# Holding back two late products and norming the last group tile by tile, at the end of a Mamba and LoRA layer kernel

## The reference

```
a   = layernorm(x)
h   = a + mamba2(rmsnorm(a))                   # stage A
mlp = h + down(silu(gate(rmsnorm(h))) * up(..))   # stage B, inner width 1792
x1  = x + layernorm(mlp)                       # stage C from here
h3  = layernorm(x1)
u   = h3 @ W_up.T + LoRA of the expert with the highest logit (4 experts, rank 8)
out = x1 + layernorm(u)
```

## Time and profile before

| | us |
|---|---|
| median of 3 runs (lowest, highest) | 816.61 (816.28, 816.96) |
| the profiled execution, its own time | 815.18 |
| its span, first to last instruction | 813.3 |
| TensorE matmuls busy | 762.6 (94%) |
| VectorE busy | 485.3 (60%) |
| ScalarE busy | 331.6 (41%) |
| GpSimd busy | 154.1 (19%) |

### The profile page before, as it was taken

One profiled execution on the slowest core, in us unless ns is written; L12 is line 12 of the kernel. 1 busy time (PEld: TensorE's weight loads), 2 busy tenths in 40 slices (PEclk: granted clock), 3 DMA queues, 4 the chain that ended last, 5 costly groups with the idle time before them and its releaser, 6 DMA issues.

```text
span 813.3 us, 13857 instructions
## 1 busy us (share of the span) xinstructions
PE 762.6 (94%) x5558; PEld 536.6 (66%) x5558; DVE 485.3 (60%) x1109; ACT 331.6 (41%) x603; POOL 154.1 (19%) x197
## 2 busy tenths in 40 slices
PE   3994989989999999999999999999999999999945
PEld 3863866668666876577666876677656866577622
DVE  6877567877644765467645765467635664265163
ACT  2643476625523363325523363325523463222201
POOL 1421121205110331115110331015110330010010
PEclk9896899999999999999999999999999999999987
DMA  9941000110103120210103020310103010111010
GB/s 325 387 160 26 2 27 1 32 47 5 49 1 65 40 52 1 49 57 13 40 1 79 27 53 1 52 53 25 30 1 78 27 27 1 27 53 27 1 52 27
DMA packets 59936, 41.11 MB, mean 51 GB/s; under 512 B 45664, under 2 KB 45792, under 8 KB 59872
## 3 DMA queue, kind: packets, MB, share of 16 engines
q1 hardware_dynamic: 59872, 40.22, 17.6%
HBM read 25.01 MB, written 4.19 MB: 36 GB/s over the span
## 4 chain that ended last, share of the span: by engine, by line
PE 85%; DVE 7%; ACT 2%; DMA 2%; issue 1%; SPq 1%; POOL 0%; POOLq 0%; DVEq 0%; ACTq 0%
PE gu L1251 34%; PE wa L1251 25%; PE acc L1251 18%; PE wc L1251 7%; DVE weights L870 2%; DMA weights<-in_w_in 1%; DVE sg L1043 1%; DVE stats_c L885 0%; PE wa L1274 0%; DVE h L1073 0%; DMA xa<-in_x 0%; DMA ht<-ra 0%; ACT act L680 0%; PE wc L1466 0%; ACT weights L560 0%
## 5 line engine op out<-in xcount | busy, mean ns | idle before, releaser
L1251 PE MATMUL gu<-h2t,weights 128*128 128x256 f16 x2688 | 313.4, 273 | 0.6 <-DVE h2t L1037 0.6
L1251 PEld LDWEIGHTS gu<-h2t,weights 128*128 128x128 f16 x2688 | 260.9, 98 | 56.1 <-issue 19.7
L1251 PE MATMUL acc<-weights,act 128*128 128x512 f16 x672 | 163.4, 379 | 6.5 <-DVE act L1048 6.5
L1043 DVE SCALAR_TENSOR_TENSOR sg<-gu,bound,sg 128x256 f32<-128x256 f32 x112 | 53.6, 479 | 122.6 <-ACT sg L670 121.9
L670 ACT ACTIVATE sg<-gu,scale_inv 128x256 f32<-128x256 f32 x112 | 52.9, 472 | 160.3 <-PE gu L1251 160.1
L1251 PE MATMUL wa<-ht,weights 128*128 128x256 f16 x912 | 110.4, 280 | 3.7 <-DMA ht<-ra 3.7
L1251 PEld LDWEIGHTS acc<-weights,act 128*128 128x128 f16 x672 | 65.3, 98 | 63.6 <-DVE act L1048 8.3
L1251 PEld LDWEIGHTS wa<-ht,weights 128*128 128x128 f16 x912 | 91.6, 101 | 22.4 <-DMA ht<-ra 4.0
L680 ACT ACTIVATE act<-sg 128x256 f16<-128x256 f32 x112 | 46.6, 416 | 88.7 <-DVE sg L1043 88.7
L1048 DVE TENSOR_TENSOR act<-sg,act 128x256 f16<-128x256 f32 x112 | 50.5, 451 | 54.0 <-ACT act L680 54.0
L943 DVE SCALAR_TENSOR_TENSOR xbc<-wa,conv_ws,xbc 128x253 f32<-128x253 f32 (+1 forms) x132 | 57.3, 475 | 10.2 <-ACT xbc L597 8.6
(11 more groups left out here) (194 smaller groups left out, 800.4 us busy)
## 6 DMA issues: line engine op xcount, KB each, us to landing
xa<-in_x SPq DMA_DIRECT2D x8, 512.0 KB, 3.6
weights<-in_x SPq DMA_DIRECT2D x8, 512.0 KB, 3.7
out_x<-h SPq DMA_DIRECT2D x16, 256.0 KB, 2.2
weights<-in_w_in SPq DMA_DIRECT2D x5, 512.0 KB, 7.0
weights<-in_w_down SPq DMA_DIRECT2D x3, 768.0 KB, 14.1
weights<-in_w_gate SPq DMA_DIRECT2D x2, 1024.0 KB, 12.3
weights<-in_w_up SPq DMA_DIRECT2D x2, 1024.0 KB, 13.8
weights<-in_w_gate SPq DMA_DIRECT2D x2, 768.0 KB, 13.8
```

Source lines behind the costliest of these rows:

```text
L1043: nc.vector.scalar_tensor_tensor(sg[:, f % 2], GU[f % 2][:, SEQ:2 * SEQ], up_to_act, sg[:, f % 2], ALU.mult, ALU.mult).then_inc(sem("prod_ ...
L1251: return nc.tensor.matmul(dst, left, right, start=start, stop=stop)
```

## The change

Four things change, in steps 8 and 9 only.

- Group 6's linear and LoRA products (`c_u(6, 0)` and `c_u(6, 1)`) leave blocks 10 and 11. TensorE makes them after the last down product, one after the other, into the banks `WA[0]` and `WA[1]`. Their copy on ScalarE, and `c_stats3(6)` and `c_out(6)` on VectorE, move behind the last block as well.
- Stage C of group 7 is written out in a function `last()` for each engine. Its norms go tile by tile, with the buffers `xa` (for x1), `hn` (for h3 and the output) and the small ones of stage A.
- Its transposes put all four column blocks of one tile in a bank; the split and the logits follow per tile. The linear product of tile 1 is cut in two halves, with the small transposes between them.
- SP loads x for group 7's stage C into `xa`, ahead of the stores of group 6.

The diff, cut to its core:

```
+def held(g):
+    return g == GROUPS - 2
 def u_bank(g, j):
-    return ACC[j] if alone(g) else WC
+    return ACC[j] if alone(g) else WA[j] if held(g) else WC
+def h3_of(g):
+    return hn if alone(g) else h3
+def x1_of(g):
+    return xa if alone(g) else x1
+T3_LAST = [WC, GU[0]]
+LAST = GROUPS - 1
...
 @block.sync
     def c_x(g):
-        if g > 0:
+        if alone(g):
+            sp.wait_ge(sem("h0_ready"), g * 2 + 2)
+        elif g > 0:
             sp.wait_ge(sem("out_ready"), g * 2)
         if g == 0:
             wait_split(sp, order)
-        sp.dma_start(x1[:], x_g[g]).then_inc(xc_loaded, 16)
+        sp.dma_start(x1_of(g)[:], x_g[g]).then_inc(xc_loaded, 16)
...
+        if b is not None and alone(b):
+            c_x(b)
         if c is not None:
             c_store(c)
-        if b is not None:
+        if b is not None and not alone(b):
...
 @block.gpsimd
-        nc.gpsimd.tensor_tensor(dst, dst, c_half[:, 0:TILES], ALU.pow).then_inc(ready, 1)
+        nc.gpsimd.tensor_tensor(dst, dst, c_half[:, 0:dst.shape[1]], ALU.pow).then_inc(ready, 1)
...
+    def last_norm(n, j, scale):
+        pool.wait_ge(sem("last_stats_ready"), 2 * n + j - 1)
+        inv_std(chain_last, s_a[:, 0, j:j + 1], mv_a[:, j, 1:2], 1.0 / scale ** 2, EPS / scale ** 2,
+                sem("last_rstd_ready"))
...
+    def last():
+        chain_last.group(0)
+        for j in range(TILES):
+            last_norm(1, j, 1.0)
+        for j in range(TILES):
+            last_norm(2, j, ACT_SCALE)
+        norm_c(LAST - 1, 3, 1.0)
+        chain_c.close()
+        for j in range(TILES):
+            last_norm(3, j, 1.0)
+        chain_last.close()
...
 @block.scalar
+    def last_t3(j):
+        eng.wait_ge(sem("last_t3_ps_ready"), j + 1)
+        eng.wait_ge(sem("u_ps_ready"), LAST * 2)
+        nc.scalar.activation(h3t[:, 0, :, j * P:(j + 1) * P], T3_LAST[j][:].rearrange("p (k q) -> p k q", k=KB),
+                             ACT.Copy).then_inc(sem("last_t3_hi"), 1)
...
+    C_AT = {4: lambda g: c_hi3(g), 7: lambda g: c_zt(g),
+            10: lambda g: held(g) or c_u(g, 0), 11: lambda g: held(g) or c_u(g, 1)}
...
+    def last():
+        for j in range(TILES):
+            c_u(LAST - 1, j)
+        for j in range(TILES):
+            last_t3(j)
+        c_zt(LAST)
+        for j in range(TILES):
+            c_u(LAST, j)
...
 @block.vector
+    def last_stats(src, j):
+        chain_last(nc.vector.bn_stats(stats_a[:, j], src[:, j]))
+        nc.vector.bn_aggr(mv_a[:, j], stats_a[:, j]).then_inc(sem("last_stats_ready"), 1)
+    def last_center(n, j, src, ready):
+        dve.wait_ge(sem("last_rstd_ready"), 2 * n + j - 1)
+        nc.vector.tensor_scalar(hn[:, j], src[:, j], mv_a[:, j, 0:1], s_a[:, 0, j:j + 1],
+                                ALU.subtract, ALU.mult).then_inc(ready, 1)
+    def last_x1(j):
+        last_center(1, j, mlp, sem("last_n1_ready"))
+        if j == 0:
+            dve.wait_ge(xc_loaded, GROUPS * 16)
+        dve.wait_ge(sem("last_n1_ready"), j + 1)
+        nc.vector.tensor_tensor(xa[:, j], xa[:, j], hn[:, j], ALU.add).then_inc(sem("last_x1_ready"), 1)
+        dve.wait_ge(sem("last_x1_ready"), j + 1)
+        last_stats(xa, j)
+    def last_t3(j):
+        dve.wait_ge(sem("last_t3_hi"), j + 1)
+        nc.vector.tensor_tensor(h3t[:, 1, :, j * P:(j + 1) * P], T3_LAST[j][:].rearrange("p (k q) -> p k q", k=KB),
+                                h3t[:, 0, :, j * P:(j + 1) * P], ALU.subtract).then_inc(sem("last_t3_split"), 1)
+    def last_out(j):
+        last_center(3, j, hn, sem("last_n3_ready"))
+        dve.wait_ge(sem("last_n3_ready"), j + 1)
+        nc.vector.tensor_tensor(hn[:, j], hn[:, j], xa[:, j], ALU.add).then_inc(sem("out_ready"), 1)
...
+    C_AT = {0: lambda g: c_stats1(g), 1: lambda g: c_x1(g), 3: lambda g: c_stats2(g), 4: lambda g: (c_h3(g), c_lo3(g)),
+            6: lambda g: c_route(g), 12: lambda g: held(g) or c_stats3(g), 13: lambda g: held(g) or c_out(g)}
...
+    def last():
+        chain_last.group(0)
+        for j in range(TILES):
+            b_mlp(LAST, j)
+            dve.wait_ge(sem("mlp_ready"), LAST * 2 + j + 1)
+            last_stats(mlp, j)
+        for j in range(TILES):
+            last_x1(j)
+        for j in range(TILES):
+            last_center(2, j, xa, sem("last_h3_ready"))
+        c_stats3(LAST - 1)
+        chain_c.close()
+        for j in range(TILES):
+            last_t3(j)
+        chain_c.group(LAST)
+        c_route(LAST)
+        c_out(LAST - 1)
+        for j in range(TILES):
+            dve.wait_ge(sem("u_ready"), LAST * 2 + j + 1)
+            last_stats(hn, j)
+        for j in range(TILES):
+            last_out(j)
+        chain_last.close()
...
 @block.tensor
+    def last_t3(j):
+        pe.wait_ge(sem("last_h3_ready"), j + 1)
+        if j == 0:
+            pe.wait_ge(sem("zt_ready"), LAST * 2)
         else:
+            pe.wait_ge(sem("prod_ready"), LAST * FBLK + FBLK - 1)
+        for k in range(KB):
+            last = nc.tensor.transpose(T3_LAST[j][:, k * P:(k + 1) * P], hn[:, j, k * P:(k + 1) * P], ident[:])
+        last.then_inc(sem("last_t3_ps_ready"), 1)
...
     def c_logits(g):
-        if alone(g):
-            pe.wait_ge(sem("h3t_ready"), 2)
-        else:
+        if not alone(g):
             pe.wait_ge(h3t_loaded, g * 32 + 32)
             prev(g, 2, 2, pe, sem("u_ready"))
         if g + 2 < GROUPS:
             pe.wait_ge(sem("dtv_ready"), g + 3)
         n = E + E * R
         for j in range(TILES):
+            if alone(g):
+                pe.wait_ge(sem("last_t3_split"), j + 1)
...
+    def c_linear(g, j, ks=range(KB)):
+        split_product(u_bank(g, j)[:], [tokens(h3t, k, j) for k in ks],
+                      [[Wh[:, S_LIN + k, s] for s in range(2)] for k in ks], start=ks[0] == 0, stop=False)
...
     def c_u(g, j):
-        if alone(g):
+        if j == 0:
             pe.wait_ge(sem("zt_ready"), g * 2 + 2)
-        elif j == 0:
-            pe.wait_ge(sem("zt_ready"), g * 2 + 2)
-            c_linear(g, j)
-        else:
+        elif not held(g):
             pe.wait_ge(sem("u_ready"), g * 2 + 1)
-            c_linear(g, j)
+        c_linear(g, j)
         c_lora(g, j)
...
+    def last():
+        for j in range(TILES):
+            c_u(LAST - 1, j)
+        for j in range(TILES):
+            last_t3(j)
+        c_logits(LAST)
+        pe.wait_ge(sem("mlp_ready"), GROUPS * 2)
+        c_linear(LAST, 0)
+        c_linear(LAST, 1, (0, 1))
+        c_zt(LAST)
+        c_linear(LAST, 1, (2, 3))
+        pe.wait_ge(sem("zt_ready"), GROUPS * 2)
+        for j in range(TILES):
+            c_lora(LAST, j)
...
+    C_AT = {6: lambda g: c_logits(g), 7: lambda g: c_zt(g),
+            10: lambda g: held(g) or c_u(g, 0), 11: lambda g: held(g) or c_u(g, 1)}
```

More of the change, by code:

```diff
@@ L503, in norm_c @@
                         sem("rstd_c_ready"))
+            def last_norm(n, j, scale):
+                pool.wait_ge(sem("last_stats_ready"), 2 * n + j - 1)
+                inv_std(chain_last, s_a[:, 0, j:j + 1], mv_a[:, j, 1:2], 1.0 / scale ** 2, EPS / scale ** 2,
+                        sem("last_rstd_ready"))
             def step(a, b, c):
+                if c is not None and alone(c):
+                    return
                 if c is not None:
@@ L522, in step @@
                     a_rms(a)
-                if c is not None:
+                if c is not None and not held(c):
                     norm_c(c, 3, 1.0)
                     chain_c.close()
+            def last():
[9 more added lines that the diff above has]
+                chain_last.close()
             def first():
@@ L538, in _ @@
             steps(step)
+            last()
         @block.scalar
@@ L710, in _ @@
             NEXT_AT = {10: lambda g: a_hi1(g), 13: lambda g: a_conv(g, 0)}
-            C_AT = {4: lambda g: (c_t3(g, 0), c_t3(g, 1)) if alone(g) else c_hi3(g), 7: lambda g: c_zt(g),
-                    10: lambda g: c_u(g, 0), 11: lambda g: c_u(g, 1)}
+            C_AT = {4: lambda g: c_hi3(g), 7: lambda g: c_zt(g),
[8 more added lines that the diff above has]
+                    c_u(LAST, j)
             def step(a, b, c):
+                if c is not None and alone(c):
+                    return
                 if a is not None:
@@ L1049, in b_lo, with b_mlp @@
                     .then_inc(sem("act_ready"), 1)
-            def b_mlp(g):
-                if g == 0:
+            def b_mlp(g, j):
+                if g == 0 and j == 0:
                     wait_split(dve, order)
[L1054 to L1058, removed]
-                    else:
-                        dve.wait_ge(sem("down_done"), g * FBLK + FBLK)
-                    nc.vector.scalar_tensor_tensor(mlp[:, j], ACC[j][:], inv_down, h1b[:, j], ALU.mult, ALU.add)\
-                        .then_inc(sem("mlp_ready"), 1)
+                if j == 0:
+                    dve.wait_ge(sem("h1b_ready"), g + 1)
+                    prev(g, 32, 32, dve, h3t_loaded)
```

(20 more changed lines are left out.)

47 lines of the change are left out of this document (8 added, 39 removed).

## The result

The changed kernel took 806.27 us, the median of 4 runs (805.04 to 807.84), against 816.64 for the kernel before in the same session: a ratio of 0.9875, 95% interval 0.9859 to 0.9891, so 10.4 us less. The forecast was 806.6. A second session (6 runs, 804.55 to 808.73, before 815.15) gave 806.28, ratio 0.9892 (0.9874 to 0.9909). The runs of the changed kernel scatter by 2.8 us in the first session and by 4.2 in the second; those of the kernel before do so as well, by 3.4 us beside the first experiments (813.77 to 817.17).

The account below looks back on a forecast made before the run. TensorE's products bound the kernel until the last down products, then the order of work across engines in the last 31 us. Gains 7.47 + 0.8 + 1.1 + 1.2 + 0.4 = 11.0, less 1.1 for clock, about 10.0: 806.6 us, range 804.6 to 809.1.

Parts of the forecast that it names:

- Held products: Group 6's late products leave TensorE before the last down product: 6.25 us, plus 1.2 from VectorE's queue.
- Norms by tile: Last group's norms one tile at a time: 0.8 us gained up to the centred tiles, 0.4 at the end.
- GpSimd beside VectorE: Roots on GpSimd stretch beside VectorE work in the last group's norms: 1.0 us together, bounds 0 and 1.3.
- Transposes, split, logits: Last group, centred pair to end of logits: 3.2 us instead of 4.3, 1.1 gained, with group 6's statistics in between.
- Last products: TensorE works through 24 linear and 2 LoRA products after the logits; stretch before first output shortens by 1.2 us.
- The clock: TensorE's granted clock falls in the thin tail and returns at 789.7, losing 1.1 us; bounds 0 and 2.6.
- rival B: Clock falls and stays low until 792.6 in the tail, costing 2.6 us: 808.2 us; chance 0.12.
- rival A: Clock holds through the tail: 805.6 us, or 804.6 with roots unstretched; chance 0.33.
- The argument from the pause of 2.51 us: A 2.51 us TensorE pause earlier in the trace, between dense work, did not lower the clock.
- Moved DMAs: Reload of x on SP's queue ahead of group 6's stores, issued about 742, some 36 us early: free.
- Rival D: Reload of x stays stuck on SP behind group 6's stores: 18 us lost, 11 gained, 823.6 us; chance 0.02.
- Rival C: Tile by tile brings nothing because each hand-over to GpSimd stands open: 7.5 of 10.0 left, 809.1 us; chance 0.09.

Follow-up runs that it names:

- the first experiments: The session in which norms in pairs, fill, statistics later and a kernel without held products ran beside the kernel before, which took 815.25 us.
- fill: Changed kernel plus ten unread matmuls behind the held products, between the last transposes and ahead of the logits: 803.34 us, ratio 0.9850 to before; repeat 803.63.
- the repeat: The changed kernel itself run once more, unaltered, in a second session: 806.28 us, ratio 0.9892 to the kernel before.
- norms in pairs: Changed kernel with the last group's three norms taking both tiles at a time again, in the same new buffers: 808.75 us, ratio 0.9919 to before.
- session II: The second of three experiment sessions; the kernel before took 815.15 us in it, the changed kernel 806.28.
- the fill with the statistics later: Changed kernel with both the ten unread matmuls and group 6's statistics behind the two last splits on VectorE: 803.20 us, ratio 0.9856 to before.
- statistics later: Changed kernel with group 6's statistics on VectorE behind the last group's two splits instead of ahead of them: 804.69 us, ratio 0.9868 to before.

## Why the prediction was right, and where it was off

*Held products: right.* 6.25 us of products and the 1.2 us of VectorE's output work, less 0.7 for the split, make 6.8; the runs gave 6.9. TensorE did not wait in blocks 10 to 13, and the held products ran in the shadow of VectorE's norms.

*Norms by tile: right, the last one undersized.* The prediction had 0.8 us gained to the centred tiles and 0.4 at the end. The traces show 0.8 and 1.2 (8.7 us before, 7.5 after).

*GpSimd beside VectorE: the mechanism right in two norms, the term too large.* The root on the path took 0.39 and 0.56 us, so 0.2 was lost to its centring, not 0.35. The end's 0.66 was not there: root 1 took 0.19 and 0.62 us from 801.07 to 801.96, though the centring (801.02) and the add (801.60) ran beside it, and the centring of tile 1, in VectorE's order behind an add, could not start before 802.21. Roots of one column took 0.55, not 0.69. The step that failed is "Tile 1's third has a centring and an add beside it: bounds 0 and 0.85 (0.44 + 0.41); I take 0.66": the stretch was 0.07 us, and hidden. The two powers that stretched to 1.08 and 0.99 us were hidden, as predicted.

*Transposes, split, logits: right.* 3.25 us from the centred pair to the last logits' end, predicted 3.2. Group 6's statistics did stand ahead of the splits.

*Last products: right at full clock.* With fill, 18 products took 3.89 us; I had 18 times 0.223, 4.0.

*The clock: the fall was right, its size was not.* The prediction had a fall and a loss of 1.1 us, with rival B at 2.6 and rival A at none. In the profiled execution the clock fell at 787.4 and came back at about 794.2; the 18 products lost 2.3 us. With the 2.02 us taken off that is a return at 792.2, which is rival B (back at 792.6, 2.6 us lost), and the repeat's trace shows the same. So the step "from 786.4 this gives 789.7" failed: the low clock lasted 6.8 us, not 3.3.

*So the forecast of 806.6 met 806.27 in part by luck.* The prediction's tail from the sum on was 27.2 us at full clock (775.02 to 802.25) and 28.3 with the fall. The traces have 26.28 with fill and 28.66 without: the last norm was 0.9 us shorter than forecast, the clock cost 2.4 us instead of 1.1, and the two errors nearly cancel. Rival B had the clock right and, with the same 0.9 us too much in its last norm, the time wrong. Rival A, 805.6 or 804.6 with the clock held, is what the fill makes of the kernel, and that took 803.3 to 803.6.

*The argument from the pause of 2.51 us fell.* The same pause in the changed kernel (TensorE, step 1, which the change does not touch):

```profile
115.32 2.74 PE L1343 MATMUL acc<-weights,act 128*128 128x512 f16 x6 [2.50 <-DVE act L1097]
```

It was 2.50 us long, and the clock was at 0.50 from 115 to 118 (windows above). In the trace before it was not, though the pause was 2.51:

```profile
115.00:118.00 3.00, 3.00 (x17) 1.80 (x16) 2.52 (x5) 1.61 (x5) 0.00 (x0) 1.00 0.58 178
```

Six down products took 2.74 us instead of the 1.47 of the earlier trace rows. Over the whole body this cost 0.75 us (661.92 against 661.17 with fill), and the execution was 1.27 us behind the one with fill when these products began; the two make the 2.02. Where the 1.27 come from was not followed up. A pause that leaves the clock alone in one execution can be followed by a low clock in another: 3 of the 13 profiled executions had it. The prediction should have taken this pause as possible in either way.

*Moved DMAs: right.*

```profile
744.29 0.58 SPq L394 DMA_DIRECT2D xa<-in_x  x1
...
802.32 1.52 SPq L405 DMA_DIRECT2D out_x<-hn  x2
```

The reload of x was issued at 744.29, 37 us before the add at 781.05 wanted it. Rival D did not happen. Rival C did not either: the traces with norms in pairs show 1.6 us for the tiles at the low clock and 2.1 with fill.

The terms as measured: held 6.9, tiles 2.1; the two make 9.0 of the 10.4. The rest, 1.4, was not tested by itself; tile-wise transposes and the order of the last products are argued causes. Body and tail together account for 9.6 us between the traces of before and changed, the 0.75 of step 1's clock left aside; so only 0.6 us needs such a cause, and the other 0.8 lies within the scatter of the executions.

The best kernels have the fill, at 803.2 to 803.6 us, with ratios of 0.985 to 0.986 against the changed kernel's 0.9875 and 0.9892. In session II, where both stood, the fill with the statistics later took 803.20 and the changed kernel 806.28. Moving group 6's statistics gave nothing more.

## What to carry to other kernels

In a pipeline's last step, look for work of the step before that nothing needs soon, and put it where the engine will wait anyway; check that its consumer's place in every other engine's queue moves along. Where a tail alternates between engines, tiles hide the hand-overs only if the next tile's work is longer than the hand-over (here 2.2 us against some 1.1). And when TensorE is thin ahead of a dense stretch on the path, price the clock: ten unread matmuls in the pauses took 2.4 us off the tail. And before a difference between executions is put down to the changed part, look at when that part began: here the two profiled executions of the changed kernel differed by 0.9 us, and all of it lay some 660 us ahead of the tail.

## What the runs showed of the hardware

- After the same TensorE pause of 2.5 us, with the same work on both sides, the granted clock was low in one execution (0.50 from 115 to 118) and not in another (1.00). It was low in 3 of 13 profiled executions, and cost 0.75 us there. The thin stretch of the tail (bursts of 0.66 us, pauses up to 1.4) was followed by a low clock in all three profiled executions that have it (changed twice, statistics later), for 6.8 us each.
- A power of one column on GpSimd took 0.55 us, of two columns 0.69; beside VectorE's add and statistics 1.08 and 0.99. The small multiply went from 0.19 to 0.39 beside a centring, whose input is one SBUF tensor, in two norms; in the third it took 0.19 beside one that had begun 0.05 us earlier, and the power 0.62. The Trainium skill (GPSIMD Engine Reference, section 1, Specifications) says that VectorE instructions in a 2-port mode contend too. The trace does not show the mode of a centring; the 0.39 fits that sentence and the 0.19 of the third norm does not.
